# Transposes with 32-bit one-pass operands in an attention and expert kernel, with a scaled difference to the former transposes added to the output

## The reference, cut to what matters

```python
x  = hidden_states                      # 1 x 4096 x 256
xn = layernorm(x)
# attention: 8 heads of 32, chunks of 12 queries that see 24 keys, relative positions
q, k, v = xn @ Wq.T, xn @ Wk.T, xn @ Wv.T
logits  = tanh((q k^T + rel_shift(q rel_k^T)) / 50) * 50
attn_out = (softmax(logits) @ v) @ Wpost.T
# experts: 8 experts of width 704, each token goes to its best 2
normed = rmsnorm(xn, norm_weight)
combine = top-2 of softmax(normed @ router.T), made to sum to 1
moe = sum_e combine[e] * ((silu(normed @ gate_e.T) * (normed @ up_e.T)) @ down_e.T)
return x + attn_out + xn + alpha * moe
```

## Time and profile before

| | us |
|---|---|
| median of 2 runs | 862.19 (861.61 to 862.78) |
| profiled execution | 869.74 |
| its span | 867.9 |
| PE busy | 807.0 (93%) |
| PE weight loads busy | 776.1 (89%) |
| DVE / ACT / POOL busy | 439.1 / 388.7 / 400.3 |

### The profile page before, as it was taken

The page is one execution under the profiler, slowest core; times in us unless marked ns, Lnnn a source line. Parts: engine busy times, 40 slices in busy tenths (PEclk is TensorE's granted clock), DMA queues, the critical chain, the costliest instruction groups (busy, mean ns, idle before and its releaser), DMA issues.

```text
span 867.9 us, 19555 instructions
## 1 busy us (share of the span) xinstructions
PE 807.0 (93%) x6503; PEld 776.1 (89%) x6503; DVE 439.1 (51%) x1037; ACT 388.7 (45%) x663; POOL 400.3 (46%) x304
## 2 busy tenths in 40 slices
PE   0678999999999999989999999999999999999994
PEld 0668999999999999888999999999999999999993
DVE  3625236777888544434444444444444444444442
ACT  4266558877666678722222332223222233222330
POOL 1138566777857566722333333333433333333332
PEclk9969689999999999979999999999999999999998
DMA  9515865988876443210236355255264363222211
GB/s 280 201 56 188 283 220 180 297 278 290 271 247 201 129 143 109 62 33 19 38 65 186 78 134 145 38 139 140 38 164 116 67 177 82 35 38 37 35 26 23
DMA packets 69217, 114.77 MB, mean 132 GB/s; under 512 B 11640, under 2 KB 52516, under 8 KB 69124
## 3 DMA queue, kind: packets, MB, share of 16 engines
q0 software_dynamic: 18304, 39.47, 17.8%
q1 hardware_dynamic: 34692, 44.66, 17.2%
q10 hardware_dynamic: 16128, 29.36, 11.8%
HBM read 66.57 MB, written 46.93 MB: 131 GB/s over the span
## 4 chain that ended last, share of the span: by engine, by line
PE 68%; POOL 10%; ACT 8%; issue 7%; DVE 3%; ACTq 2%; DMA 2%; SPq 0%; POOLq 0%; DVEq 0%
PE psum L1117 58%; POOL w_ring L523 5%; PE psum L1206 5%; POOL arena L557 4%; ACT psum L711 2%; PE psum L1172 2%; PE psum L1265 2%; ACT arena L687 2%; ACT arena L715 1%; PE psum L1133 1%; DMA out<-spare,sca_i 1%; ACT w_ring L651 1%; ACTq L629 1%; DMA arena<-xn_all 1%; POOL arena L515 1%
## 5 line engine op out<-in xcount | busy, mean ns | idle before, releaser
L1117 PE MATMUL psum<-w_ring,xT 128*128 x1608 | 276.1, 327 | 3.9 <-DVE xT L1005 3.7
L1117 PEld LDWEIGHTS psum<-w_ring,xT 128*128 128x128 f32 x1608 | 257.0, 188 | 15.4 <-issue 15.4
L570 POOL DMA_INDIRECT out<-spare,sca_i x67 | 106.6, 1590 | 281.3 <-DVE spare L1104 261.8
L1117 PE MATMUL psum<-w_ring,hT 128*128 x1139 | 152.7, 288 | 1.9 <-DVE spare L1104 1.4
L996 DVE TENSOR_TENSOR spare<-psum,spare 128x704 f32<-128x704 f32 x67 | 59.7, 891 | 164.6 <-PE psum L1117 164.6
L1117 PEld LDWEIGHTS psum<-w_ring,hT 128*128 128x128 f32 x1139 | 140.6, 190 | 2.3 <-issue 2.3
L759 ACT ACTIVATE spare<-psum 128x704 f32<-128x704 f32 x67 | 50.8, 758 | 159.9 <-PE psum L1117 159.9
L668 ACT ACTIVATE xT<-psum,nwp 128x128 fp32r<-128x128 f32 x134 | 41.9, 363 | 172.4 <-PE psum L1172 169.8
L557 POOL TENSOR_TENSOR arena<-arena,const 120x540 f32<-120x540 f32 x38 | 64.4, 1694 | 103.5 <-ACT arena L715 103.5
L1117 PE MATMUL psum<-arena 32*120 32x108 f32 (+1 forms) x1216 | 92.1, 281 | 0.0
L1117 PEld LDWEIGHTS psum<-arena 32*120 32x120 f32 (+1 forms) x1216 | 84.1, 185 | 8.8 <-issue 1.0
(11 more groups left out here) (161 smaller groups left out, 994.5 us busy)
## 6 DMA issues: line engine op xcount, KB each, us to landing
w_split<-w_ring POOLq DMA_DIRECT2D x20, 1088.0 KB, 8.0
w_ring<-w_split SPq DMA_DIRECT2D x40, 544.0 KB
raw<-in_w_raw ACTq DMA_DIRECT2D x32, 544.0 KB, 4.9
nrm_d<-x_all ACTq DMA_DIRECT2D x8, 512.0 KB, 5.5
arena<-xn_d SPq DMA_DIRECT2D x34, 120.0 KB
arena<-in_x SPq DMA_DIRECT2D x37, 108.0 KB
out<-arena SPq DMA_DIRECT2D x37, 108.0 KB
bd_d<-arena SPq DMA_DIRECT2D x38, 84.4 KB
```

Source lines behind the costliest of these rows:

```text
L570: pool.indirect_dma_start(out=out, out_offset=bass.IndirectOffsetOnAxis(ap=sca_i[:, b:b + 1], axis=0), in_=y[:, b % 2, :], in_offset=None, ...
L1117: return pe.matmul(out_ap, lhs, rhs, start=first, stop=last)
```

## The change

The transposes take their operands as float32r instead of float32: the same bytes in SBUF seen by a second name (`xg_m`, `xn_m`, `win_m`, `o_m`, `spread_m`, `hb_m`), PSUM seen as float32r, and the identity and both permutations copied once into a float32r tile, `turns`. These two copies stand at the head of VectorE's program, behind the arrival of the constants.

For the gathered tokens the float32 transposes stay as well: `turn_x` makes 2 transposes in the new form and then 2 in the former one into the other half of the bank. VectorE copies 64 columns of the former result, subtracts the same columns of the new one from it, and only then raises `s_xtl`; the difference, times 2^20, is added to the first 64 columns of `y` in `weigh`. So `s_y` now counts two per block.

```diff
+        turns = sb("turns", [P, P + 2 * GK], F32R)
+        ident_m = turns[:, 0:P]
+        perm_in = turns[0:GK, P:P + GK]
+        perm_out = turns[0:GK, P + GK:P + 2 * GK]
...
             link(dve.memset(rel_bd[:, :, :, :], 0.0))
+            dve.wait_ge(s_const, 16)
+            dve.tensor_copy(ident_m, ident).then_inc(s_turns, 1)
+            dve.tensor_copy(turns[:, P:P + 2 * GK], const[:, C_IN:C_IN + 2 * GK]).then_inc(s_turns, 1)
 
             dve.wait_ge(s_dim, 16 * HC)
...
-                ins.then_inc(s_xtl, 1)
+                if b >= 4:
+                    dve.wait_ge(s_y, 2 * (b - 3))
+
+                dve.tensor_copy(both[:, b % 4, :], psum[:, x_bank(b), D:D + CMP]).then_inc(s_bth, 1)
+                dve.wait_ge(s_bth, b + 1)
+                dve.tensor_tensor(both[:, b % 4, :], both[:, b % 4, :], psum[:, x_bank(b), 0:CMP], ALU.subtract).then_inc(s_xtl, 1)
...
                 dve.tensor_scalar(y[:, b % 2, :], psum[:, 6, 0:D], slot_w[:, b:b + 1], None, ALU.mult).then_inc(s_y, 1)
+                dve.wait_ge(s_y, 2 * b + 1)
+                dve.scalar_tensor_tensor(out=y[:, b % 2, 0:CMP], in0=both[:, b % 4, :], scalar=float(2 ** 20),
+                                         in1=y[:, b % 2, 0:CMP], op0=ALU.mult, op1=ALU.add).then_inc(s_y, 1)
...
-                    ins = pe.matmul(psum[:, 2, k * GK:(k + 1) * GK], win[0:GK, window(g), k * P:(k + 1) * P], perm_in,
+                    ins = pe.matmul(moved(psum[:, 2, k * GK:(k + 1) * GK]), win_m[0:GK, window(g), k * P:(k + 1) * P], perm_in,
                                     start=True, stop=True, is_transpose=True)
...
-                    ins = pe.transpose(psum[:, x_bank(b), k * P:(k + 1) * P], xg[:, b % NXG, k * P:(k + 1) * P], ident)
+                    ins = pe.transpose(moved(psum[:, x_bank(b), k * P:(k + 1) * P]), xg_m[:, b % NXG, k * P:(k + 1) * P],
+                                       ident_m)
+                for k in range(KD):
+                    ins = pe.transpose(psum[:, x_bank(b), D + k * P:D + (k + 1) * P], xg[:, b % NXG, k * P:(k + 1) * P],
+                                       ident)
                 ins.then_inc(s_xt, 1)
...
-                    ins = pe.transpose(psum[:, 4 + c // 3, (c % 3) * P:(c % 3 + 1) * P], hb[:, b % 2, c * P:(c + 1) * P],
-                                       ident)
+                    ins = pe.transpose(moved(psum[:, 4 + c // 3, (c % 3) * P:(c % 3 + 1) * P]),
+                                       hb_m[:, b % 2, c * P:(c + 1) * P], ident_m)
                 ins.then_inc(s_ht, 1)
```

More of the change, by code:

```diff
@@ L67 @@
 OOB = 2 * T
+CMP = 64
 ALPHA_LO, ALPHA_HI = -0.5, 2.0
@@ L135, in program @@
         in_use = sb("in_use", [1, 2], I32)
+        xg_at = cursor[0]
         xg = sb("xg", [P, NXG, D])
@@ L142, in program @@
         mask = const[0:GK, C_MASK:C_MASK + GQ]
-        perm_in = const[0:GK, C_IN:C_IN + GK]
-        perm_out = const[0:GK, C_OUT:C_OUT + GK]
+        turns = sb("turns", [P, P + 2 * GK], F32R)
+        xg_m = sb("xg_m", [P, NXG, D], F32R, at=xg_at)
+        ident_m = turns[:, 0:P]
+        perm_in = turns[0:GK, P:P + GK]
+        perm_out = turns[0:GK, P + GK:P + 2 * GK]
         ring_at = cursor[0]
@@ L154, in program @@
         xn_all = sb("xn_all", [P, TT, D], at=ring_at)
+        xn_m = sb("xn_m", [P, TT, D], F32R, at=ring_at)
         x_all = sb("x_all", [P, TT, D], at=ring_at + 2 * 2 * WC * 4)
+        spare_at = cursor[0]
         spare = sb("spare", [P, 15, D])
@@ L168, in program @@
         arena = sb("arena", [P, sum(sizes.values())])
-        at, off = {}, 0
+        arena_m = sb("arena_m", [P, sum(sizes.values())], F32R, at=arena_at)
+        at, at_m, off = {}, {}, 0
         for name, n in sizes.items():
             at[name] = arena[:, off:off + n]
+            at_m[name] = arena_m[:, off:off + n]
             off += n
         win = at["win"].rearrange("p (b d) -> p b d", b=NWIN + 1)
+        win_m = at_m["win"].rearrange("p (b d) -> p b d", b=NWIN + 1)
+        o_m = at_m["o"].rearrange("p (h n) -> p h n", h=H)
+        spread_m = at_m["rep"].rearrange("p (h a r n) -> p h a r n", h=H, a=2, n=CHUNK)
         xw = at["xw"].rearrange("p (b d) -> p b d", b=NXW)
@@ L195, in program @@
         hb = spare[:, 6:12, :].rearrange("p t n -> p (t n)")[:, 0:2 * HIDP].rearrange("p (b n) -> p b n", b=2)
+        hb_m = sb("hb_m", [P, 2, HIDP], F32R, at=spare_at + 6 * D * 4)
         y = spare[:, 12:14, :]
+        both = spare[:, 14, :].rearrange("p (b n) -> p b n", b=4)
         mv = sb("mv", [P, TT, 2])
@@ L219, in program @@
         s_const = sem("s_const")
+        s_turns = sem("s_turns")
+        s_bth = sem("s_bth")
         s_dim = sem("s_dim")
@@ L567, in scatter @@
             def scatter(b):
-                pool.wait_ge(s_y, b + 1)
+                pool.wait_ge(s_y, 2 * b + 2)
                 pool.wait_ge(s_sc, 16 * b)
@@ L1117, in mm, with moved @@
                 return pe.matmul(out_ap, lhs, rhs, start=first, stop=last)
+            def moved(out_ap):
+                return out_ap.bitcast(F32R)
             def logits(t):
@@ L1132, in logits @@
                     for k in range(KD):
-                        ins = pe.transpose(psum[:, 4, D + k * P:D + (k + 1) * P], xn_all[:, t, k * P:(k + 1) * P], ident)
+                        ins = pe.transpose(moved(psum[:, 4, D + k * P:D + (k + 1) * P]), xn_m[:, t, k * P:(k + 1) * P], ident_m)
                     ins.then_inc(s_nt, 1)
@@ L1213, in down @@
                 if b:
-                    pe.wait_ge(s_y, b)
+                    pe.wait_ge(s_y, 2 * b - 1)
                 slot = slots[b] if b < NB_MIN else pe.value_load(blk_slot[0:1, b:b + 1], min_val=0, max_val=NRING - 1)
@@ L1264, in scores @@
                     for k in range(KD):
-                        pe.matmul(psum[0:GK, i, k * GQ:(k + 1) * GQ],
-                                  spread[0:GQ, HC * k + i, :, :, :].rearrange("p a r n -> p (a r n)"),
-                                  ident[0:GQ, 0:GQ], start=k == 0, stop=False, is_transpose=True)
+                        pe.matmul(moved(psum[0:GK, i, k * GQ:(k + 1) * GQ]),
+                                  spread_m[0:GQ, HC * k + i, :, :, :].rearrange("p a r n -> p (a r n)"),
+                                  ident_m[0:GQ, 0:GQ], start=k == 0, stop=False, is_transpose=True)
                 for k in range(KD):
@@ L1277, in turn_out @@
                 for k in range(KD):
-                    ins = pe.matmul(psum[:, 6, k * GK:(k + 1) * GK],
-                                    o_sb[0:GK, HC * k:HC * (k + 1), :].rearrange("p h n -> p (h n)"), perm_out,
+                    ins = pe.matmul(moved(psum[:, 6, k * GK:(k + 1) * GK]),
+                                    o_m[0:GK, HC * k:HC * (k + 1), :].rearrange("p h n -> p (h n)"), perm_out,
                                     start=True, stop=True, is_transpose=True)
@@ L1324, in _ @@
             pe.wait_ge(s_const, 16)
+            pe.wait_ge(s_turns, 2)
             turn(0)
```

## The result

The changed kernel takes **915.38 us** (median of 2 runs, 915.04 to 915.73), against 862.19: a ratio of **1.059**, 95% interval 1.051 to 1.066. The forecast was 871, with a range of 858 to 907. The forecast was wrong: the change is slower by 53 us, where 9 were expected.

A forecast was written before the change was run, and what follows sets the result against it. It took each block to end in a latency chain from the tokens' transposes through ScalarE and VectorE, with TensorE outside the ring in many attention steps. 14 + 0.5 - 7 + 1.5 = +9 us on 862.19 gave 871, range 858 to 907.

The forecast's parts named there:

- Part 1: TensorE transposes: a one-pass transpose of 128 columns costs 0.060 us instead of 0.110; its data load doesn't bind.
- the first rival: Transposes get no faster, by data load or two passes; only the additions remain: 906 us, chance 0.15.
- Part 2: Loop over blocks: faster transposes -0.39, added former pair +0.22, copy and subtraction +0.39 us a block; +14 us over 65 blocks.
- Rival 2: Loop over blocks: the latency chain isn't what bounds a block, there is half a microsecond of slack: 846 us, chance 0.08.
- Part 3: Attention: shorter transposes count only in steps that TensorE heads and half the router's: -7 us, ends -12 and -3.
- Rival 3: The clock falls as PE idles some 0.6 of 7.2 us in each block: over 900 us, chance 0.04.
- Part 4: Kernel start: VectorE takes up `q_scale` 2.2 us later, behind the constants and two copies: +1.5 us, between 0 and 2.2.

The follow-up runs named there:

- the tokens first: Kernel before the change, with TensorE transposing the next block's tokens ahead of the hidden values in each turn: 854.96 us, ratio 0.976.
- after: The changed kernel, one-pass transposes plus the comparison, against the kernel before the change: 915.38 us, ratio 1.059.
- the kernel with this part alone: Against the changed kernel: one-pass transposes in attention only, former ones in the block loop, no comparison: 889.18 us, ratio 1.019.
- before: The kernel without the change: 862.19 us in the two runs beside the changed kernel, mean 866.0 over 31 fast runs beside the experiments.
- the register load first: The changed kernel with ScalarE's register load put ahead of its wait for the tokens' transposes, from block 2 on: 878.35 us, ratio 1.000.
- the kernel with the tokens first and one-pass blocks: Kernel before, tokens transposed ahead of hidden values, one-pass transposes in blocks only, no comparison, identity copies later on VectorE: median 844.48 us.

## Why the prediction was wrong, step by step

**Part 1 failed in its size.** It took 0.060 us for a one-pass transpose of 128 columns, between 55 and 66 ns, from the passes of the matmul; the runs give 0.087 where TensorE is the bound, 0.085 in the stream. The pass was right: 0.06 is what the two transposes take right behind the long matmuls, in the chain of the kernel with the tokens first, and in the trace of after the first two gaps among the hidden values' six are 0.059 and 0.063 us (medians), the later ones 0.085. So the term that was mis-sized is the load of the data, put at "about 60 ns in a stream" on the ground that its record is 50 ns shorter than an ordinary one. Nothing in the trace bounded that from above but 0.093, the pace of the 120-column loads, and that bound should have been the upper end. From 0.085 upwards, the prediction itself says, the first rival decides. It did: the loop was priced there at 65 x (0.61 - 0.20) = 27 us, and it took 65 x 0.42 = 27. The rule of the Trainium skill that the prediction set aside (TensorE: Matmul & The Clock Gate, LDWEIGHTS: P / 1.2 ns) is off in its number, since it gives 107 ns for 128 columns where 85 were measured in the stream. By it nothing would be gained; 0.023 us per transpose were, where 0.050 were forecast.

That the load paces the new form can be read from three shapes in the trace of after, at the full clock (medians). With 128 columns loaded the gap is 0.085 us, whether 128 columns move (block loop) or 120 (the windows). Those of the windows follow the two of the attention output, and the gaps of the four are 0.059, 0.064 and 0.085, the pattern of the block loop again. With 120 loaded and 108 moving it is 0.081 between the later ones of the scores. The former transposes went by the moving columns instead: 0.109, 0.102 and 0.092. No run changed the load alone, so it stays an inference.

**Part 2 held in all but that.** The added former pair was priced at 0.22 and the copy and subtraction at 0.39, 0.61 a turn; with former transposes alone the turn rose by 0.597. Rival 2, that the latency chain isn't the bound, fell with two runs: tokens first (0.23 us a turn back), and the register load first. What the prediction missed in the chain is ScalarE's register load. It named the span from 602.44 to 603.03 between the transposes and the rounding and did not ask what filled it. In the changed kernel it kept its old length of 0.28; where it grew, it can account for the half of what the transposes gave that is missing.

**Part 3 failed, and by far the most.** Its work was rather better than forecast, -10 us at the full clock, the later start included, where -7 was taken. But the step asked only what each transpose costs and which steps TensorE heads, and not what the slices at half clock in the earlier trace rows would do. Time at half clock went from 46 to 105 us in after, 106 in the kernel with this part alone, and that is 30 us. It was a term put at nothing without a reason. Rival 3 had the mechanism, put it into the loop over blocks, where the clock stayed at 1.00 even with 26 us of idle TensorE, and gave it 0.04.

**Part 4.** The start was put at +1.5 between 0 and 2.2. In the changed trace VectorE took up `q_scale` at 7.40 instead of 5.32, and the first transfers of the normalised x into the windows were issued at 15.73 instead of 15.09: +0.64.

**The sum**, in us:

| | forecast | measured | from |
|---|---|---|---|
| loop, comparison | +40 | +39 | 65 x 0.597 |
| loop, new form | -26 | -11 | 65 x (7.40 - 7.573) |
| attention, start, last output | -5 | -10 | one-pass in attention alone, at the full clock |
| clock | 0 | +30 | half of 59 us more at half clock |
| together | +9 | +48 | 913.5 - 866.0 = 47.5 |

The miss in these means is 39 us: 30 by the clock and 15 by the new form in the loop, less 6 that the other terms came out better. The remaining 5 to 6 of the 44 us between 871 and 915 come from the reference: at 843 us for the full clock, the two runs that gave 862 had some 34 us at half clock (an estimate from their time), where the mean of before is 46.

**What stays open.** Which property of the former transposes keeps the clock up, where doubled one-pass transposes or ordinary matmuls do not, isn't settled: doubling also stretched the steps, to 23 to 45 us over before at the full clock, and no run held these apart. Nor is it shown why the register load lasts 0.28 in one kernel and 0.4 to 0.5 in another; an overlap with TensorE's own load is not enough. In the kernel with the tokens first and one-pass blocks the 25 loads that overlap it last 0.57 and the 38 that don't 0.28, but in before all of them overlap it and the median is 0.28.

## What to carry to other kernels

Split every time by the granted clock before reading it: within one kernel the span followed the time at half clock by 0.52 us per us, and what was left scattered by 2.5 us where the raw times scattered by 30. Where a profile shows slices at half clock, a change of TensorE's work there can cost more than it saves (here 30 us against 10), so try it first where the clock stands at 1.00 or near it (the blocks, the later steps) and measure the rest by itself. When the chain over TensorE has slack hidden beside it, name everything in the gap between two engines, register loads too: moving one of them ahead of its wait was worth 0.58 us a turn, and swapping two stages 0.23.

## What the runs showed of the hardware

- In a stream, one-pass transposes of float32r data come 0.085 us apart with 128 columns moving and 128 loaded, and 0.081 with 108 moving and 120 loaded; the former ones 0.109 and 0.092. Right behind matmuls of 352 columns two of them come 0.06 apart. Over a whole turn halving the passes gained 0.023 us of 0.110, 21%.
- TensorE idle for 26 of 448 us in the loop, a piece in every turn, kept the full clock. In attention, one-pass transposes up to step 13 took the time at half clock from 46 to 94 us, those from step 14 on only to 54. Doubled former ones brought it to 30; doubled one-pass ones left it at 97, ordinary one-pass matmuls beside them at 110.
- A register load on ScalarE with what follows it up to the first activation stands for 0.57 us in a chain, though its own record is 0.28. Its median went from 0.28 to 0.41 and 0.49 us in kernels that differ from before by the transposes and the comparison.
